# The Laplacian of the last three chunks of edge maps: from VectorE to TensorE, with the identity and minus four times it

## The reference, cut to what matters

```python
sobel_h = dwconv(x, K_SX)
sobel_v = dwconv(x, K_SY)
sobel = jnp.sqrt(sobel_h ** 2 + sobel_v ** 2 + 1e-08)
lap = jnp.abs(dwconv(x, K_LAP))          # 0 1 0 / 1 -4 1 / 0 1 0
diag = jnp.maximum(jnp.abs(dwconv(x, K_D1)), jnp.abs(dwconv(x, K_D2)))
grad = jnp.sqrt(sobel ** 2 + lap ** 2 + 1e-08)
E = jnp.stack([sobel, lap, diag, grad])
y = jnp.einsum('kbchw,koc->kbohw', E, w_branch) + b_branch[:, None, :, None, None]
...
feat = jax.nn.gelu(y, approximate=False)
```

## Time and profile before

| | us |
|---|---|
| median of 3 runs | 4693.0 |
| lowest, highest | 4685.66, 4695.4 |
| the profiled execution's own time | 4680.56 |
| its span, first to last instruction | 4678.8 |
| TensorE busy | 4404.2 |
| VectorE busy | 2834.5 |
| ScalarE busy | 2209.3 |
| GpSimd busy | 1240.7 |

### The profile page before, as it was taken

How to read it: one execution, slowest core, us unless ns; L and a number is a source line. 1 busy time by engine, 2 the same in 40 slices (tenths; PEclk the granted TensorE clock), 3 DMA queues, 4 the chain that set the end, 5 groups by cost and what they waited for, 6 DMA issues and landing times. The chain is left out here.

```text
span 4678.8 us, 76658 instructions
## 1 busy us (share of the span) xinstructions
PE 4404.2 (94%) x27368; PEld 3565.6 (76%) x27368; DVE 2834.5 (61%) x4120; ACT 2209.3 (47%) x3983; POOL 1240.7 (27%) x1030
## 2 busy tenths in 40 slices
PE   8999999999999999999999998689989999999968
PEld 6887988888888888878879888556666676666626
DVE  4354454354454454544544543289789979978996
ACT  3343343343343333433433433056666666667666
POOL 2442442433433424424424333000020030002003
PEclk9999999999999999999999999799999999999979
DMA  6685685786776766766856866867466646746613
GB/s 197 225 292 202 238 294 201 242 274 219 247 258 227 259 238 233 276 217 239 296 202 235 281 213 207 291 212 262 150 201 219 227 155 213 262 150 201 203 54 128
DMA packets 486678, 1045.80 MB, mean 224 GB/s; under 512 B 40624, under 2 KB 94512, under 8 KB 484016
## 3 DMA queue, kind: packets, MB, share of 16 engines
q1 hardware_dynamic: 486320, 1040.99, 65.8%
HBM read 665.02 MB, written 375.82 MB: 222 GB/s over the span
## 5 line engine op out<-in xcount | busy, mean ns | idle before, releaser
L818 POOL TENSOR_TENSOR toeplitz<-taps 128x512 f32<-128x512 f32 x768 | 896.8, 1195 | 869.3 <-PE bank L488 801.3
L488 PEld LDWEIGHTS bank<-toeplitz,columns 128*128 128x128 f32 x8192 | 956.2, 192 | 14.3
L488 PE MATMUL bank<-toeplitz,columns 128*128 128x128 f32 x8192 | 957.0, 275 | 0.0
L394 PE MATMUL bank<-x_hi,w_hi 128*128 128x512 f32 x1536 | 611.6, 398 | 16.9 <-DVE x_lo L665 16.3
L396 PE MATMUL bank<-x_lo,w_hi 128*128 128x512 f32 x1536 | 599.8, 391 | 0.0
L395 PE MATMUL bank<-x_hi,w_lo 128*128 128x512 f32 x1536 | 599.3, 390 | 0.0
L1541 POOL TENSOR_TENSOR centred<-centred,x_out 128x512 f32<-128x512 f32 x128 | 174.4, 1384 | 1602.1 <-ACT centred L1324 1600.5
L752 DVE TENSOR_SCALAR ckey_t<-bank 128x256 f32<-128x256 f32 x256 | 108.4, 424 | 781.9 <-PE bank L488 781.9
L1174 PE MATMUL bank<-edge,w_branch 128*128 128x512 f32 x1024 | 482.5, 621 | 77.4 <-ACT edge L1272 77.4
L478 PE MATMUL bank<-loaded,toeplitz 128*128 128x256 f32 x2048 | 499.3, 387 | 48.0 <-DMA loaded<-tiles_dram 44.8
L665 DVE TENSOR_TENSOR x_lo<-x_sb,x_hi 128x1536 fp32r<-128x1536 f32 x128 | 251.6, 1966 | 410.5 <-ACT x_hi L534 410.5
(11 more groups left out here) (143 smaller groups left out, 6896.2 us busy)
## 6 DMA issues: line engine op xcount, KB each, us to landing
x_sb<-in_x_tiled SPq DMA_DIRECT2D x128, 1024.0 KB, 6.2
loaded<-tiles_dram SPq DMA_DIRECT2D x256, 433.5 KB, 5.5
tiles_dram<-tiles SPq DMA_DIRECT2D x112, 867.0 KB, 7.2
inverse<-inverse_dram SPq DMA_DIRECT2D x256, 256.0 KB, 8.0
att_dram<-out_hi SPq DMA_DIRECT2D x256, 256.0 KB, 4.0
att_dram<-out_lo SPq DMA_DIRECT2D x256, 256.0 KB, 5.5
att_hi<-att_dram SPq DMA_DIRECT2D x64, 1024.0 KB, 7.6
att_lo<-att_dram SPq DMA_DIRECT2D x64, 1024.0 KB, 9.9
```

The source lines that it names most:

```text
L394: nc.tensor.matmul(banks[t][:, :], wh, xh, start=(k == 0), stop=False)
L488: last = nc.tensor.matmul(bank[:, v * M:(v + 1) * M], columns[:, h % 2, t - T_K, v + b, a * HT:(a + TO) * HT], w[:, t, d, :], start=(d == ...
L818: last = nc.gpsimd.tensor_tensor(toeplitz[:, h % 2, t, :].rearrange("p (d o r) -> p d o r", o=HD, r=PL), tap, point, ALU.mult)
```

## The change

In the three steps without a projection, VectorE leaves out its three Laplacian instructions (`stencils` returns after the diagonal). TensorE makes the same sum in the free bank `P_BANKS[k]` with four f32 matmuls of 512 columns, in `laplace`: the identity times the row above, the row below and `side`, and minus four times the identity times the centre. The operands are the rows of `xb` themselves (64 of every 66 floats). ScalarE's `laplacian` then reads the bank instead of `edge`.

The matrices live in `diagonals`, which lies over the start of `att_hi`. SP loads the identity into it at the start of step j = 5, once all projections are done, ahead of the row loads of that step; VectorE makes the multiple by minus four after k = 0 of that step. TensorE's order in a step is `laplace(0)`, `laplace(1)`, `branch(0)`, `laplace(2)`, `branch(1)`, `laplace(3)`, `branch(2)`, `branch(3)`. `xb_used[k]` is now counted up by the last matmul of `laplace`, and VectorE waits for the `laplace` of the k before ahead of its first instruction, because `side` is one buffer.

```diff
 (sync: step)
+                    if pj is None and prev_p is not None:
+                        sp.wait_ge(projected, KT * B * NCH)
+                        sp.dma_start(diagonals[:, 0, :], io["ident"]).then_inc(ident_loaded, 16)
                     if rows:
 (tensor)
+                def laplace(b, j, k):
+
+                    u = chunk(b, j)
+                    x = xb[:, k, :].rearrange("p (r w) -> p r w", w=W2)
+                    if j == NCH - LAG:
+                        pe.wait_ge(summed, KT * (B * NCH - 1) + k + 1)
+                    else:
+                        pe.wait_ge(done["edges"], START + KT * (u - 1) + k + 1)
+                    pe.wait_ge(diagonals_ready, 1)
+                    for name in ("side", "dx", "smooth"):
+                        pe.wait_ge(done[name], KT * u + k + 1)
+                    parts = ((0, x[:, 0:CR, 1:W + 1]), (0, x[:, 2:XR, 1:W + 1]), (0, side[:, 1:XR - 1, :]), (1, x[:, 1:XR - 1, 1:W + 1]))
+                    for i, (d, part) in enumerate(parts):
+                        last = nc.tensor.matmul(P_BANKS[k][:, :], diagonals[:, d, :], part, start=(i == 0), stop=(i == len(parts) - 1))
+                    last.then_inc(xb_used[k], 1)
+
                 def step(pj, mj, slot, prev_p, prev_m, fresh):
                     ...
+                        if pj is None and k < KT:
+                            laplace(*mj, k)
                         if mj is not None and k >= 1:
 (scalar)
-                def laplacian(u, k, s):
+                def laplacian(u, k, s, alone):
+                    source = P_BANKS[k][:, :] if alone else edge[:, s, 1, :]
                     act.wait_ge(xb_used[k], START + u + 1)
-                    nc.scalar.activation(lap_sq[:, s, :, :], edge[:, s, 1, :].rearrange("p (r w) -> p r w", w=W), ACT.Square
+                    nc.scalar.activation(lap_sq[:, s, :, :], source.rearrange("p (r w) -> p r w", w=W), ACT.Square
                                          ).then_inc(done["squares"], 1)
-                    nc.scalar.activation(edge[:, s, 1, :], edge[:, s, 1, :], ACT.Abs)
+                    nc.scalar.activation(edge[:, s, 1, :], source, ACT.Abs)
 (vector)
-                def stencils(b, j, k, follows):
+                def stencils(b, j, k, follows, alone):
                     ...
                     dve.wait_ge(xb_loaded[k], 16 * u + 16)
+                    if alone and (k >= 1 or j > NCH - LAG):
+                        dve.wait_ge(xb_used[(k - 1) % KT], START + u + min(k, 1))
                     nc.vector.tensor_tensor(side, x[:, :, 0:W], x[:, :, 2:W2], ALU.add).then_inc(done["side"], 1)
+                    if alone:
+                        dve.wait_ge(done["diag"], n - 1)
                     ...
                     nc.vector.tensor_tensor(maps_of[:, 2, :, :], dx[:, 2:XR, :], dx[:, 0:CR, :], ALU.subtract).then_inc(done["diag"], 1)
+                    if alone:
+                        return
                     ...
                 def step(pj, mj, slot, prev_p, prev_m, fresh):
                     ...
-                            stencils(*mj, k, k >= 1 or prev_m is not None)
+                            stencils(*mj, k, k >= 1 or prev_m is not None, pj is None)
+                            if pj is None and k == 0 and prev_p is not None:
+                                dve.wait_ge(ident_loaded, 16)
+                                nc.vector.tensor_scalar(diagonals[:, 1, :], diagonals[:, 0, :], -4.0, None, ALU.mult
+                                                        ).then_inc(diagonals_ready, 1)
```

More of the change, by code:

```diff
@@ L887, in edges @@
         hidden = sb("hidden", [HID, 1])
+        with nc.sbuf_tensor("diagonals", [P, 2, P], F32) as diagonals:
+            pass
         att_hi, att_lo = (ctx.enter_context(nc.sbuf_tensor(f"att_{n}", [P, 2, HALF, CH], F32R)) for n in ("hi", "lo"))
@@ L907, in edges @@
         mean_w_set = sem("mean_weights_set")
+        ident_loaded = sem("edge_ident_loaded")
+        diagonals_ready = sem("diagonals_ready")
         w_proj_loaded = [sem(f"edge_w_proj_loaded{i}") for i in range(2)]
@@ L1290, in step @@
                         diagonal(KT * u + k + 1, k % 2)
-                        laplacian(u, k, k % 2)
+                        laplacian(u, k, k % 2, pj is None)
                         if k == 0 and prev_m is not None:
```

## The result

The median is 4702.86 us over 20 runs, against 4694.3 us for 20 runs of the kernel before. The ratio is 1.0020, with a 95% interval of 1.0012 to 1.0028. The forecast was 4704.5 us, which over the median of 4693.0 known then is a ratio of 1.0025.

A forecast was written before the change was run, and what follows sets the result against it. VectorE was taken to set the pace in the three chunks before the change. Terms 5.2, 1.6 and 0.9 (7.7 at full clock) plus 3.4 and 0.4 for clock gave +11.5 us on 4693.0: 4704.5 us, range 4695 to 4712.

The forecast's parts named there:

- late row load: Start of step j = 5: SP's new wait delays the row loads, so VectorE's first unit starts 5.2 us later.
- first unit to third chunk's first unit, clock apart: From the end of unit 0's smoothing in j = 5 to that in j = 7: 67.2 against 65.6 us, +1.6.
- last chunk to the last branch matmul: From unit 0's smoothing in j = 7 to the last branch matmul: 37.4 against 36.5 us, +0.9.
- cold branch group at the start: Last branch group of j = 4, after 4.8 us idle, runs at 1.2 GHz: 6.8 instead of 3.4 us, +3.4.
- cold L1: Slow clock on each chunk's second Laplacian after a TensorE gap, mostly covered by 2.0 us of waiting: 0.4 us in all.
- The period: Time per chunk in the three steps without projection: 33.6 us against 32.1, although VectorE lost 8.2 us of work.
- bounds of 0 and 5: Limits in us on the slow-clock cost at the start of the phase, the upper with part of the first Laplacian.
- rival that every burst begins cold: TensorE starts every burst throttled in the three chunks: +4.8 us per chunk, +25.5 in all, 4718.5 us; chance 0.08.
- first rival: Start of the phase: clock stays up or row load is less late; +7.7 us or less, 4700.7; chance 0.27.
- faster rival: Waits for `side` and the Gelus do not stop TensorE, the only bound: -9.7 us, 4683.3 us; chance 0.05.

The follow-up runs named there:

- L0 ahead of B3: Changed kernel with the first Laplacian of steps j = 6 and 7 ahead of the previous step's last branch group on TensorE: stretch 108.07 us, 5.7 less.
- The Gelus first: Changed kernel with ScalarE's four Gelus ahead of the Laplacian's square and absolute value of unit 0: stretch 114.72 us, timed 1.0017.
- the second side buffer: Changed kernel with a second `side` tile for odd k, so VectorE waits for the Laplacian of two units before: stretch 115.78 us.
- the rows first: Changed kernel with the identity loaded behind the four row loads of step j = 5, not ahead: stretch 107.27 us, timed 1.0019.
- half a Laplacian: Changed kernel with two of each Laplacian's four matmuls left out, output not the reference's: stretch 106.04 us, 7.7 less.

## Why the prediction was right, point by point

The median came within 1.6 us of the forecast. That closeness is in part luck: single executions lie 20 us apart. The stretch is the better measure. The sum was made of five terms, and each is compared by it; the figures are the first execution's where nothing else is said.

| term | forecast, us | measured, us |
|---|---|---|
| late row load | 5.2 | 5.19 |
| first unit to third chunk's first unit, clock apart | 1.6 | 69.34 - 1.83 - 65.63 = 1.88 |
| last chunk to the last branch matmul | 0.9 | 40.66 - 39.41 = 1.25 |
| cold branch group at the start | 3.4 | 1.83, and 3.34 in the second execution |
| cold L1 | 0.4 | 0 in both (covered) |
| sum | 11.5 | 10.15; second execution 11.2 to 11.6 |

**The row load** was the largest term and is shown three ways: by the row with the DMA wait, by the wait alone in the kernel before (+4.8), and by its removal (-6.5 with the cold group, in the stretch). That the identity and its multiple are covered is shown too: L0 waits for neither.

**The period** was forecast at 33.6 and is 33.89; this and the last chunk cost 0.6 us more than forecast and the clock 2.0 less, so the terms' errors partly cancel. It was walked with a gap of 3.1 us before L1 (3.15) and of 2.0 before B0 (1.54). The chain was right: B3, L0, tail, B0. VectorE's 24.6 us were removed and gave nothing, because the Laplacian's result now arrives behind a branch group in TensorE's queue and the Gelus stand behind it in ScalarE's. The experiments bear this out. L0 ahead of B3 took 3.64 us off at each of two boundaries. The Gelus first and the second side buffer gave nothing alone, because the other wait stayed and a group behind a gap ran slow, and together they brought the period to 28.18.

**The clock** was the term least well sized. The idle of 4.6 us at the start cost 1.8 and 3.3 us in two executions, where 3.4 was forecast. Nine executions have an idle of 4.6 to 5.0 us there, and the group behind it took between 5.14 and 6.77 us: the length of the idle alone does not fix the cost, and a single number could not be right. The prediction's bounds of 0 and 5 hold. That a slow L1 is covered by the wait for B0 was right, and holds for six slow L1, three in the second execution and three with the rows first, all of 5.2 to 5.4 us, without a change of period.

**The forecast of the difference**, 0.25% against 0.20%, is within the interval of 0.12 to 0.28%. The prediction split its chances at 0.2%, which is the middle of this interval, so whether the change is slower by more or by less than that stays open. That it is slower is measured.

**The rival that every burst begins cold** came true in part. In the second execution of the changed kernel, and with the rows first, L1 was slow in every chunk. But it took 5.2 to 5.4 us and not 6.8, and B0 behind it ran in 3.67, so this rival's price of 4.8 us per chunk was not paid. B0 was the slow group, as the rival had it, only under other edits: in all three chunks of the two side buffers and in two of three with half a Laplacian.

The Trainium skill, TensorE: Matmul & The Clock Gate, HAM oscillation, describes a loop in which a wait ahead of each burst makes the next one start throttled. The traces agree in part. With the Gelus first, the first L1 behind 3.15 us of idle ran at 0.71. With the rows first, L1 behind the same idle began at 1.00 for 0.84 us and then fell to 0.50. In the first execution of the changed kernel the same idle left the clock at 1.00. The kernel before has such a row too, the burst at 4512.45, which ran at 1.00 for its first 1.05 us behind 3.57 us of idle; the prediction names it for its first rival, but its sentence that the rows agree for gaps of 3.57 us up passes over it.

**The faster rival**, TensorE as the only bound at -9.7 us, was not what happened, but it named the limit: with the rows loaded first, the Gelus first and two side buffers, TensorE is the bound and the stretch is 12.2 us under the kernel before. The rival's figure kept the late start.

## What to carry to other kernels

Work taken off the busiest engine is worth only what the chain loses. If the result comes back through another engine's queue, walk one period and ask what stands ahead of it in that queue, and what stands behind it in the queue of its reader. A new wait on the transfer queue delays every load issued after it; put the load that nobody needs yet last. And when TensorE is idle in short gaps, a repair that merges two gaps into one, or removes the cover behind a gap, can cost in clock what it gains: compare the length of the same group of matmuls before judging an order.

## What the runs showed of the hardware

In the one execution with idle matmuls on an otherwise waiting TensorE, 2.74 us of them in the gap ahead of L1, L1 took 3.67 instead of 5.2 to 5.4 us, and the time from the first L0 to the last branch matmul was 4.9 us shorter. The same gap of 3.15 us, left empty, left L1 at 3.67 us in one execution of the changed kernel and made it 5.2 to 5.4 in the other. ScalarE's square from a bank took 0.57 to 0.60 us and from SBUF 0.61 to 0.63, so the bank operand cost nothing. A Laplacian, in which three of the four f32 matmuls read rows of 64 out of 66 floats, took 3.43 to 3.45 us for eight instructions at full clock, the same as a branch group over contiguous rows.
